# FFN of an attention + gated-FFN kernel: gate and up products of a block as seven half-depth products

## What is computed

```python
xn = layernorm(x)                      # x: 2 x 512 tokens of 512 channels
s  = attention(xn, wq, wk, wv, wo)     # 32 query heads, 8 kv heads, window 128
# FFN with 4-bit-like integer weights, groups of 128 rows:
gate_proj = (gate_w - gate_z) * gate_s # 512 x 1792
up_proj   = (up_w - up_z) * up_s       # 512 x 1792
down_proj = (down_w - down_z) * down_s # 1792 x 512
f  = (silu(xn @ gate_proj) * (xn @ up_proj)) @ down_proj
out = x + s * silu(f)
```

## Time and profile before

| | us |
|---|---|
| median of 3 runs | 896.03 |
| lowest, highest | 896.02, 896.39 |
| the profiled execution, own time | 895.29 |
| its span, first to last instruction | 893.5 |
| PE busy in the span | 881.9 |
| POOL busy | 463.4 |
| DVE busy | 645.7 |

### The profile page before, as it was taken

The page is one execution under the profiler, slowest core; times in us unless marked ns, Lnnn a source line. Parts: engine busy times, 40 slices in busy tenths (PEclk is TensorE's granted clock), DMA queues, the critical chain, the costliest instruction groups (busy, mean ns, idle before and its releaser), DMA issues. The chain is left out here.

```text
span 893.5 us, 14415 instructions
## 1 busy us (share of the span) xinstructions
PE 881.9 (99%) x4414; PEld 744.2 (83%) x4414; DVE 645.7 (72%) x1065; ACT 453.9 (51%) x1250; POOL 463.4 (52%) x361
## 2 busy tenths in 40 slices
PE   8999999999999999999999999999999999999997
PEld 7778888888888888888888888888878888888885
DVE  7877787778687787778687787778655657566556
ACT  5665655565656556565655655565652212222223
POOL 4665544655455555555555545644436435435435
PEclk9999999999999999999999999999999999999999
DMA  8011110110101011110101100012316356446462
GB/s 258 25 48 39 37 33 24 36 45 26 35 23 47 23 35 35 29 41 24 35 23 47 35 23 23 23 33 74 97 46 175 100 148 176 114 133 176 121 185 94
DMA packets 84588, 61.43 MB, mean 69 GB/s; under 512 B 3665, under 2 KB 71889, under 8 KB 84561
## 3 DMA queue, kind: packets, MB, share of 16 engines
q1 hardware_dynamic: 83840, 59.98, 23.3%
q10 hardware_dynamic: 720, 1.11, 0.4%
HBM read 58.98 MB, written 2.10 MB: 68 GB/s over the span
## 5 line engine op out<-in xcount | busy, mean ns | idle before, releaser
L36 PE MATMUL ps<-xt_hi,w_lo 128*128 128x512 f32 x604 | 237.4, 393 | 0.7 <-PEq L413 0.5
L37 PE MATMUL ps<-xt_lo,w_hi 128*128 128x512 f32 x604 | 235.7, 390 | 0.0
L38 PE MATMUL ps<-xt_hi,w_hi 128*128 128x512 f32 x604 | 235.4, 390 | 0.0
L897 POOL TENSOR_TENSOR q_lo<-work,q_hi 128x512 fp32r<-128x512 f32 x64 | 82.7, 1293 | 157.8 <-ACT q_hi L769 157.8
L902 POOL TENSOR_TENSOR pt_lo<-kept,pt_hi 128x512 fp32r<-128x512 f32 x112 | 142.8, 1293 | 24.6 <-ACT pt_hi L790 24.6
L38 PEld LDWEIGHTS ps<-xt_hi,w_hi 128*128 128x128 f32 x604 | 113.4, 188 | 24.5
L36 PEld LDWEIGHTS ps<-xt_hi,w_lo 128*128 128x128 f32 x604 | 113.7, 188 | 23.4 <-issue 1.1
L37 PEld LDWEIGHTS ps<-xt_lo,w_hi 128*128 128x128 f32 x604 | 113.7, 188 | 21.3
L779 ACT ACTIVATE probs<-ps,neg_max 128x128 f32<-128x128 f32 x256 | 90.4, 365 | 53.4 <-DVE neg_max L1041 53.4
L790 ACT ACTIVATE pt_hi<-kept 128x512 fp32r<-128x512 f32 x112 | 69.2, 633 | 66.0 <-DVE kept L1051 66.0
L36 PE MATMUL ps<-wo_hi,o_lo 128*128 (+1 forms) x256 | 99.9, 390 | 0.3 <-issue 0.2
(11 more groups left out here) (99 smaller groups left out, 1734.7 us busy)
## 6 DMA issues: line engine op xcount, KB each, us to landing
work<-L_attn_wq SPq DMA_DIRECT2D x32, 256.0 KB, 2.7
work<-L_attn_wo SPq DMA_DIRECT2D x32, 256.0 KB, 2.6
work<-L_ffn_gate_w SPq DMA_DIRECT2D x14, 256.0 KB, 3.3
work<-L_ffn_gate_z SPq DMA_DIRECT2D x14, 256.0 KB, 4.2
work<-L_ffn_gate_s SPq DMA_DIRECT2D x14, 256.0 KB, 5.1
work<-L_ffn_up_w SPq DMA_DIRECT2D x14, 256.0 KB, 3.2
work<-L_ffn_up_z SPq DMA_DIRECT2D x14, 256.0 KB, 4.2
work<-L_ffn_up_s SPq DMA_DIRECT2D x14, 256.0 KB, 4.4
```

What stands on the lines that cost most here:

```text
L36: pe.matmul(out, stat[1], mov[0], start=first, stop=False)
L37: pe.matmul(out, stat[0], mov[1], start=False, stop=False)
L38: return pe.matmul(out, stat[0], mov[0], start=False, stop=last)
L897: pool.tensor_tensor(lo, row_of(unit, b, i), hi.bitcast(F32), ALU.subtract).then_inc(rope_split, 1)
```

## The change

For 10 of the 14 blocks (pairs 2 to 6, `SEVEN_FROM` = 2) the gate and up products of a block are seen as one 2x2 block product: rows are (gate, up), the depth of 512 is cut into two parts of 256, and the token columns are the two halves. Winograd's form of Strassen's scheme makes this of seven products of depth 256 (two depth tiles) instead of eight: 7 x 2 x 3 = 42 matmuls a block instead of 48. `down` keeps its 24.

The scheme needs sums of the operands:

- once, of the tokens: `x_parts` (POOL) adds `xt_hi` and `xt_lo` back together (8 additions of 128x512), `t_parts` (DVE) makes four differences in two depth tiles (8 operations), `t_hi_parts` (ACT) and `t_lo_parts` (POOL) split them (8 and 8). They are put into pairs 0 and 1, in program order between the pieces and middles that were there.
- in each block, of the weights: POOL makes four sums of 128x256 (`s_parts`), and the high and low parts of seven half-depth weight tiles take the place of those of gate and up.
- in each block, of the products: one PSUM bank (`A`, alternating) accumulates P1, P1+P6, P1+P6+P7 and the first gate half; ACT copies it out three times on the way (`copy`), and DVE adds the copies to the banks `B` and `C` (`add_up1`, `add_gate2`, `add_up2`). PE waits for each copy before it adds the next product to `A`, and puts two `down` tiles behind the fourth and two behind the fifth product.

The pairs are written out instead of looped. `tokens` and `t_parts` lie where the seven-part weights and `t_hi`/`t_lo` lie, and `res` is now `tokens`, so the load of the residual waits for the last product (`made` at 7 x 10). Weight loads of the seven-part blocks wait for `scaled` (the dequantised piece) instead of `ffn_w_split`.

```diff
+SEVEN_FROM = 2
+BLOCKS = 2 * (PAIRS - SEVEN_FROM)
...
+    def x_parts(self, pool, kt):
+        for i, (k, hf) in enumerate(((kt, 0), (kt, 1), (2 + kt, 0), (2 + kt, 1))):
...
+            pool.tensor_tensor(x[:, i, :], sh.xt_hi[:, k, cols].bitcast(F32), sh.xt_lo[:, k, cols].bitcast(F32),
+                               ALU.add).then_inc(self.x_made, 1)
+    def t_parts(self, dve, kt):
+        dve.wait_ge(self.x_made, 4 * kt + 4)
+        dve.tensor_tensor(t[:, T1, :], x[:, 1, :], x[:, 0, :], ALU.subtract).then_inc(self.t_made, 1)
...
+    def lo_up_and_gate(self, pool, blk):
+        self.split(pool, blk, U1, U2, up, sh.w_split)
+        pool.wait_ge(sh.scaled, self.index_of(blk, GATE) + 1)
+        pool.tensor_tensor(s[:, 0, :], gate[:, upper], gate[:, lower], ALU.add).then_inc(self.s_made, 1)
+        pool.tensor_tensor(s[:, 2, :], up[:, upper], gate[:, upper], ALU.subtract).then_inc(self.s_made, 1)
+        pool.tensor_tensor(s[:, 1, :], s[:, 0, :], up[:, upper], ALU.subtract).then_inc(self.s_made, 1)
+        pool.tensor_tensor(s[:, 3, :], up[:, lower], s[:, 1, :], ALU.subtract).then_inc(self.s_made, 1)
+        self.split(pool, blk, G2, G2, gate[:, lower], self.s_split)
+        for i, done in enumerate((self.s_split, sh.w_split)):
+            self.split(pool, blk, S1 + 2 * i, S2 + 2 * i, ..., done)
...
+    def products(self, pe, blk, downs):
+        pe.wait_ge(sh.w_split, self.index_of(blk, UP) + 1)
+        self.product(pe, blk, U1, a, True, self.b_of(0, 0))
+        self.product(pe, blk, U2, self.B, True, self.b_of(1, 0))
+        pe.wait_ge(self.s_split, 2 * blk + 2)
+        self.product(pe, blk, S1, self.C, True, self.t_of(T1))
+        pe.wait_ge(self.copied, 3 * blk + 1)
+        self.product(pe, blk, S2, a, False, self.t_of(T2))
+        downs(range(0, 2))
+        pe.wait_ge(sh.w_split, self.index_of(blk, GATE) + 1)
+        pe.wait_ge(self.copied, 3 * blk + 2)
+        self.product(pe, blk, S3, a, False, self.t_of(T3))
+        downs(range(2, 4))
+        pe.wait_ge(self.copied, 3 * blk + 3)
+        self.product(pe, blk, G2, a, False, self.t_of(T4))
+        pe.wait_ge(self.added, 3 * blk + 2)
+        self.product(pe, blk, S4, self.C, False, self.b_of(1, 1))
...
         def _(sp):
+            sp.wait_ge(sv.made, 7 * BLOCKS)
             sp.dma_start(res[:, :, :], x.rearrange("(t p) h -> p t h", p=P)).then_inc(res_in, 16)
...
         def _(pool):
+            for n in range(SEVEN_FROM):
+                for e in range(4):
+                    for at, kind, ii, _ahead in pieces(n, e):
+                        fw.lo(pool, n, at, kind, ii)
...
+                    split_mid(n, *ORDER[e])
+                    if (n, e) in ((0, 1), (0, 2)):
+                        sv.x_parts(pool, e - 1)
+                    if (n, e) in ((1, 0), (1, 1)):
+                        sv.t_lo_parts(pool, e)
...
         def _(dve):
+                    if n == 0 and e >= 2:
+                        sv.t_parts(dve, e - 2)
```

More of the change, by code:

```diff
@@ L31, in wait, with three_passes @@
     eng.wait_ge(sem, count)
[L34 to L38, removed]
+def three_passes(pe, out, stat, mov, first, last, grown=False):
+    pe.matmul(out, stat[1], mov[0], start=first, stop=False, skip_group_check=grown)
+    pe.matmul(out, stat[0], mov[1], start=False, stop=False, skip_group_check=grown)
+    return pe.matmul(out, stat[0], mov[0], start=False, stop=last, skip_group_check=grown)
 class Shared:
@@ L223, in ffn_block, with place, pieces, seven_beside @@
         block = ctx.enter_context(nc.Block())
[L225 to L239, removed]
+        def place(n, ii, hf):
+            return (0, 3 + n % 2)[hf] if ii == 0 else 1 + hf
+        def pieces(n, e):
+            return [(at, *IN_BODY[at]) for at in BESIDE[e] if not (n == 0 and at < EARLY)
+                    and not (n == SEVEN_FROM - 1 and at >= 3)]
+        def seven_beside(e):
+            return {2: ((0, UP),), 3: ((0, GATE), (-1, DOWN))}.get(e, ())
         @block.sync
         def _(sp):
-            def body(n, last):
+            for n in range(SEVEN_FROM):
                 for e in range(4):
-                    for at, kind, ii, ahead in pieces(n, last, e):
-                        if first(n) and at < EARLY_LOADS:
+                    for at, kind, ii, ahead in pieces(n, e):
+                        if n == 0 and at < EARLY_LOADS:
                             continue
-                        fw.load(sp, n, at, kind, ii, n + ahead if ahead else n)
-            over_pairs(sp, body)
+                        fw.load(sp, n, at, kind, ii, n + ahead)
+            for blk in range(-1, BLOCKS):
+                if blk + 1 < BLOCKS:
+                    fw.load_next(sp, sv.index_of(blk + 1, UP), UP, blk + 1)
+                    fw.load_next(sp, sv.index_of(blk + 1, GATE), GATE, blk + 1)
+                fw.load_next(sp, sv.index_of(blk, DOWN), DOWN, blk)
+            sp.wait_ge(sv.made, 7 * BLOCKS)
             sp.dma_start(res[:, :, :], x.rearrange("(t p) h -> p t h", p=P)).then_inc(res_in, 16)
@@ L1165 @@
     from concourse.bass_utils import run_bass_kernel_spmd
[L1167 removed]
+    nc = bacc.Bacc("TRN2", target_bir_lowering=False, num_devices=1, dynamic_dma_scratch_size=8192)
     arrays = {name: np.ascontiguousarray(a) for name, a in inputs.items()}
```

350 lines of the change are left out of this document (299 added, 51 removed).

## The result

The changed kernel takes **902.97 us** (median of 4 runs, 902.29 to 904.79) against 896.02 (895.47 to 896.39): a ratio of 1.0081, 95% interval 1.0064 to 1.0099, so slower by 5.7 to 8.9 us. The forecast was 902.2. The profiled execution's own time is 902.61 with a span of 900.6, where before it was 895.29 and 893.5.

What follows compares the result with a forecast made beforehand. PE was taken to bound the kernel, its FFN stretch without a gap. Terms -13.6 + 10.3 + 4.7 + 2.4 + 0.2 + 2.2 = +6.2 us on 896.0 gave 902.2; the forecast's own range was 899 to 907.

Steps and rivals of the forecast that it cites:

- Removed: PE's queue in the FFN: 6 matmuls fewer in each of 10 blocks, 60 x 0.2268 = 13.6 us saved.
- The two waits for pair 1's pieces: Head of the FFN: PE waits 1.5 us for the gate piece and longer for the up piece, together 10.3 us.
- the rival in which turns cost nothing: POOL's queued additions escape the 1.70 us turns with DVE; up product at 690.9, total 897.2; 13%.
- The clock: Behind the up piece's wait PE returns at half clock: 2.2 us lost, between 0 and 3.3.
- The first seven-part block: PE waits there for first product, third product, down piece and third copy: 0.5, 2.8, 0.7, 0.7, together 4.7 us.
- 128x256 on POOL: Price of a half-size POOL operation, in no row: 0.70 us from memsets, between 0.65 and 1.29.
- The rival of a POOL-bound block: Every seven-part block: 128x256 costs nearly 1.29, shared time 17.0 against 14.97, +14 us, 916; 12%.
- Steady blocks: Blocks 1 to 9: no PE waits, cost 0; smallest slack 1.9 us, at ACT's third copy.
- The tail wait: After the last product PE waits for the first token half's SiLU, multiply and splits before down: 2.4 us.
- The residual: Late 2 MB load takes 7.2 us, so POOL's joins start later but make up a part: 0.2 us.
- faster: POOL's operations on the new tiles run at memset pace, 0.53 instead of 1.29 us: -5.3 us, 890.7; 6%.
- The change does not do what it says: Rival: PE's matmuls on the new tiles run at another distance than 0.2268 us; 2%, either way.

Runs made afterwards that it cites:

- the run at full clock: 34 and 11 idle matmuls added to the changed kernel in PE's waits for pair 1's up piece and the first seven-part block's third product: 901.16 us.
- the version without the split transfer: Changed kernel with seven-part blocks from pair 3 instead of 2 and the token work spread over pairs 1 and 2, residual in one transfer: 894.3 us.
- the last one: Seven-part blocks from pair 3, token work spread over pairs 1 and 2, plus the residual in two transfers, the first asked for earlier: 892.67 us.

## Why the prediction was right, point by point

The spans differ by 7.1 us, where the prediction's sum was 6.2.

- **Removed: 13.6.** As said: 852 matmuls, and no gap for 135 us from 740 on.
- **The two waits for pair 1's pieces: 10.3.** Measured 1.35 (681.82 after 680.35, less one distance, and 0.1 on the first matmul) and 8.5, in all 9.85. The walk had the product at 693.15; it started at 693.21. So close a match is luck, since PE's whole FFN began 0.47 us later than in the walk; the waits themselves were 0.45 shorter. Turns of 1.70 were the right model: the four additions took 6.73 us, and the rival in which turns cost nothing had the product at 690.9.
- **The clock: 2.2, ends 0 and 3.3.** For the wait that it was meant for, one distance of 0.59 and six of 0.43 cost 1.6: near the first of its two estimates (1.65). That estimate was a guess with no row of matmuls behind it, and its fit is partly luck: seven matmuls were slow here, eleven and twelve in two kernels with a shorter wait at the same place. What the term left out: the wait of 2.7 us in the first seven-part block brought the same drop and another 1.5. Net that is little, since without it the small waits of 1.2 us in all come back (the run at full clock).
- **The first seven-part block: 4.7** (0.5, 2.8, 0.7, 0.7). Measured 0.5 and 2.9; the last two were covered by the slow matmuls, and stand there when the clock holds (0.56 and 0.61 above one distance).
- **128x256 on POOL: 0.70.** It takes 0.72 to 0.76 alone, and 1.06 to 1.19 where it meets a two-SBUF operation of DVE:

```profile
728.10 0.72 POOL L371 TENSOR_TENSOR s_parts<-work,s_parts 128x256 f32<-128x256 f32 x1
728.78 0.73 POOL L352 TENSOR_TENSOR seven_lo<-gate_row,seven_hi 128x256 fp32r<-128x256 f32 x1
```

The rival of a POOL-bound block was therefore off. The estimate that the prediction made from the Trainium skill's page "GPSIMD Engine Reference" (Elementwise — side-by-side cycle accounting), 0.75, was as near as the one from the memsets.
- **Steady blocks: 0.** True, but with a slack of 1.4 us where the walk had 1.9.
- **The tail wait: 2.4.** Measured 2.4 (881.57 after 879.06, less one distance, and 0.1 on the first matmul). The working as written does not give it: its four durations and four hand-overs, less 1.36, are 2.0 and not 2.2. The chain took that long (PE was idle for 2.1), and the rest is overlap between matmuls that a wait breaks, which the prediction did not count; the two slips cancel.
- **The residual: 0.2.** This is the term that was mis-sized. The transfer took 9.1 us, not 7.2, so the joins began 2.8 us behind the first gated tile, and made up only 0.5 of it (8.70 us for the seven, 9.22 in the earlier trace rows). The rate of 406 to 410 GB/s was right; the start, put at 2 us with no row to show it, was not: the row of GB/s climbs over six slices, 3.8 us, before the rate is reached. From PE's last product the last stores were issued 18.7 us on, where before it was 14.2: 4.5 more, 2.4 of them the wait, 2.1 the residual. To the end of the span it is 3.7 more, 1.3 over the wait. Most of the 0.8 between 2.1 and 1.3 is a difference between two executions: the last stores took 3.55 us to the end of the span in the kernel before, 2.83 here and 2.8 in the kernel before with its loop written out. The trace with two transfers has the tail 2.1 shorter.
- **Not in the sum:** PE's first FFN matmul is 0.47 us later (669.61 against 669.14). The kernel before with its loop written out has it at 669.73, so it need not come of the seven products; among the changed kernel's variants this start lies anywhere from 669.4 to 670.7, once at 672.2 (the kernel without the additions), though the attention is the same in all. Its cause stays open. The first ten or so matmuls behind each wait start slightly over one distance apart, 0.2 in all.

Sum: -13.6 + 9.85 + 1.6 + 1.5 + 0.5 + 2.9 + 2.4 + 1.3 + 0.5 + 0.2 = 7.15. Against the terms of the prediction that is +1.1 for the residual, +0.7 for the last two points, +0.9 for the clock, -1.3 for the first block and -0.45 for the two waits: part of it cancels. That the forecast's median (902.2) and the measured one (902.97) are 0.8 apart owes something to that.

The other rivals: *faster*, by POOL at memset pace, fell with 1.25 us an addition. *The change does not do what it says* fell with 0.2267 us a matmul (14.96 us for a block's 66).

## What to carry to other kernels

A saving on the bounding engine is paid for by what the saving needs, and that is paid once and at one place: here eight additions and eight differences in front of two weight pieces cost almost all that 60 matmuls gave. Walk the queues of the helping engines around the insertion operation by operation, with the turns that they take, and put the preparation behind what the bounding engine asks for next, or where it has several us to spare. A buffer that is reused for a late load moves that load onto the end of the program: price the transfer with its start, or split it.

## What the runs showed of the hardware

- **The clock falls behind short waits, and not each time.** PE came back at 0.43 us a matmul (1.2 GHz) after 8.3 us idle, and after 2.73 us in the changed kernel, but not after 2.79 in the kernel without the additions. After 2.34 us it came back so in the version without the split transfer, and not in the last one. After 2.1 us in the tail it did not in the changed kernel, but did in those without the differences and with the differences moved:

```profile
881.89 0.79 PE L36 MATMUL ps<-w_hi,mid_lo 128*128 128x512 f32 x1 [2.11 <-POOL mid_lo L669]
882.48 0.63 PE L37 MATMUL ps<-w_lo,mid_hi 128*128 128x512 f32 x1
882.90 0.63 PE L38 MATMUL ps<-w_hi,mid_hi 128*128 128x512 f32 x1
```

In the kernel with idle matmuls the drop came only with the fifth matmul behind the tail's wait. Seven matmuls were slow behind each of the changed kernel's two long waits, and up to thirteen in the others. A wait of 2 to 4 us thus cost its own length, or 1.5 to 2.8 us more, from one execution to the next, where PE sets the pace; in the tail, where the residual does, the slow matmuls cost nothing. The runs of the version without the split transfer spread over 4.7 us, the shortest (892.02) with a mean granted clock of 0.998 and the longest (896.68) with 0.994; that this is the same drop in some runs and not in others fits, but was not shown, and one run of 894.30 has 0.998 too. The page "TensorE: Matmul & The Clock Gate" of the Trainium skill (Wait — 56ns, not 53.3ns?) gives 426.7 and 215.7 ns between starts for this size at the two levels; the first agrees (0.43), the second is 0.227 here, in a stream in which each matmul has its own weight load.
- **Turns hold even against a full queue.** Four POOL additions queued back to back took 6.73 us beside DVE's two-input operations and 5.02 alone. The page "SBUF — State Buffer" of the Trainium skill (SBUF: two separate sides) describes an exclusive lock for a whole instruction; the trace agrees, and shows that POOL does not keep it from one of its instructions to the next: DVE gets in between every time.
- **A lone 2 MB load** took 9.1 us and reached 406 GB/s only after 3.8 us of climbing, counted from its first bytes; 1280 KB took 6.5 us and 768 KB 4.5.
